# Cross attention: which engine shifts the second of four units, and who sums part of the first

## The reference

```python
def _L1_attn_ref(text_embeds, video_embeds, Wq, bq, Wk, bk, Wv, bv, Wo, bo):
    q = (text_embeds @ Wq.T + bq).reshape(num_texts, num_words, HEADS, HEAD_DIM)
    k = (video_embeds @ Wk.T + bk).reshape(num_vids, num_frames, HEADS, HEAD_DIM)
    v = (video_embeds @ Wv.T + bv).reshape(num_vids, num_frames, HEADS, HEAD_DIM)
    logits = jnp.einsum('avhd,bthd->abhvt', k, q) / math.sqrt(HEAD_DIM)
    weights = jax.nn.softmax(logits, axis=3)
    attn = jnp.einsum('avhd,abhvt->abhtd', v, weights)
    attn = attn.mean(axis=0)
    return attn @ Wo.T + bo
```

## Time and profile before

| | |
|---|---|
| median of three runs | 2539.25 us (2531.22 to 2540.06) |
| profiled execution | 2540.07 us, its span 2537.9 us |
| busy over the span | PE 86%, DVE 79%, ACT 69%, POOL 61% |
| cross attention | 256 chunks between about 635 and 2216 us |
| DMA in that stage | none |

### The profile page before, as it was taken

The page is one execution under the profiler, slowest core; times in us unless marked ns, Lnnn a source line. Parts: engine busy times, 40 slices in busy tenths (PEclk is TensorE's granted clock), DMA queues, the critical chain, the costliest instruction groups (busy, mean ns, idle before and its releaser), DMA issues. The chain is left out here.

```text
span 2537.9 us, 48686 instructions
## 1 busy us (share of the span) xinstructions
PE 2184.6 (86%) x12375; PEld 1531.1 (60%) x12376; DVE 2010.7 (79%) x3333; ACT 1757.8 (69%) x5024; POOL 1551.5 (61%) x1693
## 2 busy tenths in 40 slices
PE   4558088683999999999999999999999999966993
PEld 2324066672666666666666666666666666666883
DVE  5943988314999999999999999999999999856664
ACT  2234253251888888888888888888888888823773
POOL 2642812372677777677777776677677767723773
PEclk9855587695999999999999999999999999976997
DMA  6410002351000000000000000000000000034555
GB/s 210 150 26 0 0 1 68 99 150 43 0 1 0 1 0 0 0 0 0 0 0 0 0 0 0 0 0 0 0 0 0 0 0 0 0 77 102 160 152 151
DMA packets 79707, 88.54 MB, mean 35 GB/s; under 512 B 22656, under 2 KB 56448, under 8 KB 77568
## 3 DMA queue, kind: packets, MB, share of 16 engines
q1 hardware_dynamic: 61184, 66.12, 9.3%
q0 software_dynamic: 8192, 16.87, 2.4%
q10 hardware_dynamic: 10240, 4.59, 0.7%
HBM read 73.87 MB, written 13.68 MB: 34 GB/s over the span
## 5 line engine op out<-in xcount | busy, mean ns | idle before, releaser
L1841 POOL TENSOR_TENSOR attend_weights<-attend_weights,attend_scales 128x512 f32<-128x512 f32 x1024 | 1048.5, 1047 | 474.8 <-DVE attend_scales L1757 474.8
L1735 DVE TENSOR_REDUCE attend_maxima<-attend_psL 128x16 fp32r<-128x1024 f32 x512 | 623.8, 1218 | 86.7 <-PE attend_psL L1657 86.7
L1751 DVE TENSOR_REDUCE attend_sums<-attend_weights 128x16 f32<-128x1024 f32 x512 | 618.5, 1208 | 4.1 <-ACT attend_weights L1787 4.1
L1801 ACT ACTIVATE attend_turned<-attend_psT 128x512 f32<-128x512 f32 x1024 | 556.6, 600 | 6.9 <-PE attend_psT L1676 6.6
L1676 PE MATMUL attend_psT<-consts,attend_weights 128*128 128x128 f32 x4096 | 530.4, 272 | 0.9 <-POOL attend_weights L1841 0.9
L1676 PEld LDWEIGHTS attend_psT<-consts,attend_weights 128*128 128x128 f32 x4096 | 477.1, 140 | 69.7 <-POOL attend_weights L1841 3.0
L1689 PE MATMUL attend_psA<-attend_turned,attend_chunk_values 128*64 128x512 f32 x2048 | 495.9, 605 | 0.8 <-ACT attend_turned L1801 0.8
L1795 ACT ACTIVATE attend_weights<-attend_psL,attend_maxima 128x64 f32<-128x64 f32 x2048 | 448.8, 334 | 52.0 <-DVE attend_maxima L1735 52.0
L1656 PE MATMUL attend_psL<-keys,attend_q_high 128*128 (+1 forms) x1024 | 434.2, 424 | 5.6 <-ACT attend_weights L1795 4.0
L1657 PE MATMUL attend_psL<-keys,attend_q_low 128*128 (+1 forms) x1024 | 404.2, 395 | 0.0
L1787 ACT ACTIVATE attend_weights<-attend_psL 128x512 f32<-128x512 f32 x512 | 316.1, 617 | 0.0
(11 more groups left out here) (318 smaller groups left out, 2565.6 us busy)
## 6 DMA issues: line engine op xcount, KB each, us to landing
moe2mix_w_tile<-in_L_ffn_w_dram SPq DMA_DIRECT2D x72, 256.0 KB
select_xbuf<-in_x_dram SPq DMA_DIRECT2D x16, 1024.0 KB, 4.9
moe1mix_w_tile<-in_L_ffn_W_dram SPq DMA_DIRECT2D x40, 256.0 KB, 2.7
select_emb<-L_attn_video_embeds_dram ACTq DMA_DIRECT2D x16, 256.0 KB, 3.1
moe2back_back<-result SPq DMA_DIRECT2D x8, 512.0 KB, 7.2
normed<-moe2route_normed SPq DMA_DIRECT2D x4, 520.0 KB, 9.2
normed<-moe1route_normed SPq DMA_DIRECT2D x4, 512.0 KB, 4.1
moe1back_back<-result SPq DMA_DIRECT2D x4, 512.0 KB, 5.9
```

The source lines that it names most:

```text
L1735: dve.tensor_reduce(maxima[:, both, :].rearrange("p j v -> p (j v)"), psL[:, both, :].rearrange("p j (v f) -> p (j v) f", f=FR), X, ALU.ma ...
L1751: dve.tensor_reduce(sums[:, both, :].rearrange("p j v -> p (j v)"), weights[:, both, :].rearrange("p j (v f) -> p (j v) f", f=FR), X, ALU. ...
L1801: act.activation(turned[:, parity, :, j * P:(j + 1) * P], psT[:, j % 2, :].rearrange("p (k q) -> p k q", k=SUB), ACT.Copy).then_inc(turned ...
L1841: pool.tensor_tensor(w, w, scales[:, s, :, None].to_broadcast([P, VC, FR]), ALU.mult).then_inc(normalised, 1)
```

## The change

Unit 1 is shifted by VectorE in place of TensorE. VectorE's subtraction for it stands behind the reciprocal and ahead of the second maxima, and its exponential becomes the one that works in place in SBUF. For four of the eight videos of unit 0 ScalarE writes the sum of the exponentials along with them (`accum_out`), and the first sums on VectorE leave these four out: 12 values from 768 elements instead of 16 from 1024. The second sums are as before.

```diff
-            SHIFTED_BY = ("ScalarE", "TensorE", "VectorE", "TensorE")
+            SHIFTED_BY = ("ScalarE", "VectorE", "VectorE", "TensorE")
+            SUMMED = 4
...
                     def total(n, parity, pair):
-                        both = slice(4 * parity + 2 * pair, 4 * parity + 2 * pair + 2)
+                        unit = 4 * parity + 2 * pair
+                        left = slice(unit * VC + (SUMMED if SHIFTED_BY[2 * pair] == "ScalarE" else 0), (unit + 2) * VC)
                         dve.wait_ge(exped, 4 * n + (2 * pair + 6))
-                        dve.tensor_reduce(sums[:, both, :].rearrange("p j v -> p (j v)"),
-                                          weights[:, both, :].rearrange("p j (v f) -> p (j v) f", f=FR), X, ALU.add).then_inc(summed, 1)
+                        dve.tensor_reduce(sums[:].rearrange("p j v -> p (j v)")[:, left],
+                                          weights[:].rearrange("p j (v f) -> p (j v) f", f=FR)[:, left], X, ALU.add).then_inc(summed, 1)
...
                         if exists(n):
+                            subtract(n, parity, 0, exists(n - 2))
                             maximum(n, 1)
                             subtract(n, parity, 1, exists(n - 2))
...
                                 for v in range(VC):
-                                    video = slice(v * FR, (v + 1) * FR)
-                                    ins = act.activation(into[:, video], psL[:, j, video], ACT.Exp, bias=maxima[:, j, v:v + 1].bitcast(F32))
+                                    video, shift = slice(v * FR, (v + 1) * FR), maxima[:, j, v:v + 1].bitcast(F32)
+                                    if v < SUMMED:
+                                        ins = act.activation(into[:, video], psL[:, j, video], ACT.Exp, bias=shift, accum_out=sums[:, 4 * parity + j, v:v + 1])
+                                    else:
+                                        ins = act.activation(into[:, video], psL[:, j, video], ACT.Exp, bias=shift)
```

## The result

| | before | after |
|---|---|---|
| median | 2535.23 us (4 runs) | 2492.02 us (2490.39 to 2500.63, 4 runs) |
| span of the profiled execution | 2537.9 us | 2489.9 us |
| cross attention, first maxima to last reciprocal | 1584.95 us | 1545.59 us |
| a steady chunk | 6.105 us | 5.99 us |

The ratio is 0.983, 95% interval 0.981 to 0.985: faster by 43 us, where 12 us less were forecast and 2502 was the range's lower end. Of the 48 us between the two spans 39.4 lie in the stage; 8.0 lie ahead of its first maxima (622.87 against 630.89 us), in code that is the same in both kernels.

The account below looks back on a forecast made before the run. TensorE was taken to bound each chunk at 6.105 us, and VectorE at 6.07 after the change. 256 x (6.07 - 6.105) = -9 us and 3 us less at the runs took 2540.07 to 2528, range 2502 to 2568.

Parts of the forecast that it names:

- What bounds before: Cross attention before the change: TensorE bounds every chunk at 6.105 us; VectorE can do one in 5.66, 0.38 to spare.
- Step 1: TensorE per chunk: loses one 512-wide shift, 0.23 us, so its floor goes from 6.105 to 5.87.
- Step 2: VectorE per chunk: gains one 128x512 subtraction between reciprocal and second maxima, charged 0.61 us, its two waits free.
- Step 3: VectorE's first sums: 768 elements instead of 1024 save 0.27 us a chunk; VectorE's new floor 6.07.
- Step 4: ScalarE's four sums: 0.15 us extra each, 0.60 a chunk; floor 5.62, hidden under VectorE's 6.07.
- Step 5: Handoffs between engines within a chunk: none becomes late, nothing has less than 0.4 us to spare.
- Step 6: Outside the steady chunk: 3 us less over 16 runs; ScalarE late once at a batch's start in both kernels.
- VectorE is faster than its rows: Rival on VectorE: smaller gap between maxima and subtraction, chunk 5.98 us, time 2505; chance 0.13.
- Costly waits: Rival on VectorE: the new subtraction's two waits aren't free, chunk 6.15 to 6.27, time 2549 to 2579; chance 0.13.
- ScalarE as the bound: Rival on ScalarE: the extra step costs more than 0.26 us; at 0.334, chunk 6.36, time 2605; chance 0.12.
- VectorE bound already: Rival on VectorE: its idle 0.30 isn't real room, net +0.34 paid in full, +87 us, 2627; chance 0.06.
- nothing freed: Rival on TensorE: it keeps 6.105 because the mix, not the shift, holds the logits back; 2540; chance 0.08.

## Why the prediction was wrong

The mechanism was right and the size was not. The step that failed is the second, VectorE's new subtraction, a term of the sum that was taken too large; the sixth, which left a stall out of the sum as the same in both kernels, comes behind it. Within the stage 12 us less were forecast, and 39.4 came. Of the 36 us between 2528 and the measured 2492.02, 20 are the chunk's 0.08, 6 the stalls, and 8 the clock ahead of the stage, which no step had; 2 are left.

- **What bounds before.** Right. With the sums alone the chunk stayed at 6.105 and VectorE's idle grew. The reading of the disturbed chunk (5.66, then 7.40) was the row that told it, against the ranking by busy shares.
- **Step 1, TensorE's floor.** 5.87 forecast, 5.90 measured in the run without the shift. The 0.23 was the spacing of logits; the fourth unit's shift is spaced 0.21 in the same trace (1408.64 to 1408.85).
- **Step 2, the new subtraction: mis-sized.** It was charged 0.61, that of the same operation ahead of the sums; measured 0.54 to 0.55. The gap from maxima to subtraction was taken at 1.35, that of maxima which had waited for TensorE, and is 1.33 now that they no longer wait. VectorE's floor came to 6.07 and is 5.99: 0.08 a chunk is 20 us in 256 chunks, most of the miss. The clue lay in the earlier trace rows: I took 0.27 for the reciprocal from a row whose successor had 1.16 instead of 1.21 and a spacing of 1.29, and then used the steady 1.35 for that successor. The two numbers belonged to one pair of rows; with both the sum gives 6.00. The run with the subtraction ahead of the reciprocal shows that the place decides: 0.60 there.
- **Step 3, the shorter sums.** Right: 0.27 (1.13 to 0.86).
- **Step 4, the read-outs.** 0.15 taken, 0.09 measured, hidden either way.
- **Step 5, who is late next.** It came out right for four sums, yet only handoffs within a chunk were followed. With eight sums a ring over two chunks set the time; at four the same ring gives (11.99 - 4 x 0.09) / 2 = 5.82, below 5.99. "Nothing here has less than 0.4 to spare" was wrong by the step's own numbers, 3.44 against 2.64 + 0.72 = 3.36: in the changed kernel ScalarE's exponential of the second unit stands at 1428.40, right behind the end of its subtraction (1427.74 and 0.63). It costs nothing, as VectorE wants it only at 1430.22.
- **Step 6, outside the steady chunk.** The runs' own extra: 0.86 on TensorE gave way to 0.71 on VectorE, 16 x 0.15 = 2 us, 3 forecast. "At a batch's start ScalarE is late once, for both kernels" failed: the stalls are gone, 6 us in 39 (1584.95 against the 1578.86 of the sums alone). The trace of before showed them, but nothing in it showed that they could go, and why they went is open.
- Sum of the stage: 256 x 0.115 = 29.4, 2.4 and 6 make 38 of the 39.4.
- **The rivals.** "VectorE is faster than its rows" came nearest, with 5.98 a chunk, by another reason than mine: nearly all lay behind the reciprocal, not in the gap behind the maxima. Its 2505 left out the stalls. Costly waits, ScalarE as the bound, VectorE bound already and nothing freed all fell. The Trainium skill, page "Perfetto Trace Analysis", section "Identifying the Most-Contended Engine", judges TensorE by its weight loads' busy share rather than the matmuls', and so puts VectorE first in both kernels (91.60 against 65.54 before, 97.44 against 62.81 after). That doesn't fit the kernel before, where VectorE's saving of 0.27 bought nothing, and fits the changed one.
- The range ended at 2502, just below the faster VectorE's 2505, with nothing in it for the stalls or for what lies ahead of the stage. With a chunk of 5.99 and nothing else changed the forecast would have been 2508, inside.

## What to carry to other kernels

When two engines are nearly level, an edit that moves work between them pays only down to the higher of the two new floors, and its halves may each be worth nothing or a loss: work out both floors before trying one half. Take a spacing from a pair of rows whose neighbours are those of the new order, and take both of the pair's numbers. In a pipeline over chunks, add up the rings that leave one chunk and come back in a later one; an engine's sum says nothing of them.

## What the runs showed of the hardware

- On VectorE a 128x512 tensor-tensor takes up 0.545 us behind a 128x32 reciprocal and 0.60 ahead of it (rows of 0.63 and 0.68).
- A sum handed out by a 64-wide ACTIVATE is an entry of its own on ScalarE, ACTIVATION_READ_ACCUMULATOR. Its row is 0.205 on average with four sums and 0.247 with eight, of which 0.09 count: pairs are spaced 0.289, and ACTIVATEs without it 0.199.
- Reductions on VectorE are spaced 1.13, 0.86, 0.79, 0.73 and 0.59 for 1024, 768, 704, 640 and 512 elements: 1.05 ns an element.
- ScalarE can stand still for 1.6 to 2.5 us at a loop's outer turn in one version of a program and not in another with nearly the same instructions; the packets of the instruction queue tell the two apart (65 against 36, and from 960 to 2160 us 31 against none), and the cause is open.
- The clock that TensorE is granted in a short stretch can differ between executions of the same code: 0.50 or 0.84 from 160 to 180 us, with 8 us in the whole time between the two profiled executions.
